# Residual rows, normalisation, router and slot places of two token tiles computed inside the attention loop of a one-core tower kernel, and the slot table written by 4-byte scatters

## What is computed

```python
h = softmax(coeff_weight[x]) @ (bases + lang_bias) * 16 + 0.1 * lang_bias[2]       # (4, 1024, 256)
p = layernorm(h) @ Wv.T + bv                                # q = k = v = p, 16 heads of 16
h = h + (softmax(p @ p.T / 4) @ p) @ Wo.T + bo              # attention over 1024 keys
xn = layernorm(h)                                           # eps 1e-5
logits = xn @ router                                        # 8 experts
top2, idx = top_k(logits, 2); w = softmax(top2)
out = h + sum over the two: w * ((silu(xn @ w13[e][:, :512]) * (xn @ w13[e][:, 512:])) @ w2[e])
```

## Time and profile before

| | us |
|---|---|
| median of 3 runs | 1062.44 (1062.09 to 1062.56) |
| the profiled execution's own time | 1064.38 |
| its span, first to last instruction | 1060.9 |
| mean granted clock of PE | 0.907 |

### The profile page before, as it was taken

The page is one execution under the profiler, slowest core; times in us unless marked ns, Lnnn a source line. Parts: engine busy times, 40 slices in busy tenths (PEclk is TensorE's granted clock), DMA queues, the critical chain, the costliest instruction groups (busy, mean ns, idle before and its releaser), DMA issues. The chain is left out here.

```text
span 1060.9 us, 18151 instructions
## 1 busy us (share of the span) xinstructions
PE 878.6 (83%) x6059; PEld 408.3 (38%) x6095; DVE 448.8 (42%) x1019; ACT 631.4 (60%) x671; POOL 281.7 (27%) x224
## 2 busy tenths in 40 slices
PE   4384899999989989999987896054999999999996
PEld 2270112112112112211214785022666666666664
DVE  5074222221212222222113899994455444554443
ACT  0124999999999999999996066301333332333322
POOL 7621000000000000000000045901555555555553
PEclk9675999999999999999999955555999999999999
DMA  1000000000000000000000477600233333333332
GB/s 22 2 12 1 1 1 1 2 1 1 1 1 1 1 2 1 1 1 1 1 1 9 151 240 208 187 2 18 50 60 55 58 56 59 60 55 60 51 48 30
DMA packets 34649, 40.00 MB, mean 38 GB/s; under 512 B 8848, under 2 KB 30370, under 8 KB 34595
## 3 DMA queue, kind: packets, MB, share of 16 engines
q0 software_dynamic: 14176, 17.45, 11.0%
q1 hardware_dynamic: 20418, 21.84, 7.0%
HBM read 22.46 MB, written 17.33 MB: 38 GB/s over the span
## 5 line engine op out<-in xcount | busy, mean ns | idle before, releaser
L679 ACT ACTIVATE h<-PS 128x1536 f32<-128x1536 f32 x342 | 464.1, 1487 | 15.6 <-PE PS L620 11.7
L630 PE MATMUL PS<-h,va 128*32 128x512 f32 x2048 | 275.6, 610 | 5.8 <-DVE acc_s L721 5.3
L874 POOL TENSOR_TENSOR w_p<-w_raw,w_p 128x1024 bf16<-128x1024 f32 x24 | 53.2, 2236 | 545.3 <-ACT w_p L880 545.3
L1162 PE MATMUL PS<-w_p,xsT 128*128 x793 | 190.0, 382 | 2.5 <-ACT xsT L1215 0.7
L620 PE MATMUL PS<-qf,ak 32*128 32x512 bf16 x1024 | 134.6, 389 | 46.7 <-ACT h L679 42.9
L620 PEld LDWEIGHTS PS<-qf,ak 32*128 32x128 bf16 x1024 | 33.2, 91 | 283.6 <-ACT h L679 222.8
L1220 ACT ACTIVATE act_s<-PS 128x512 f32<-128x512 f32 x69 | 41.3, 598 | 154.7 <-PE PS L1162 154.7
L1125 POOL DMA_INDIRECT out<-y_s,idx_tok x68 | 107.7, 1584 | 54.7 <-issue 47.8
L1162 PEld LDWEIGHTS PS<-w_p,xsT 128*128 128x128 f16 x828 | 81.5, 98 | 86.2 <-issue 5.2
L1111 POOL DMA_INDIRECT xs<-xrows,idx_tok x70 | 73.2, 1046 | 129.5 <-DVE weight L1259 85.3
L1179 PE MATMUL PS<-w_p,hidT 128*128 x828 | 101.7, 273 | 0.3 <-DVE hidT L1278 0.3
(11 more groups left out here) (259 smaller groups left out, 865.1 us busy)
## 6 DMA issues: line engine op xcount, KB each, us to landing
w_raw<-w SPq DMA_DIRECT2D x24, 512.0 KB, 4.8
out<-h SPq DMA_DIRECT2D x8, 512.0 KB, 2.9
xrows<-x_parts SPq DMA_DIRECT2D x8, 512.0 KB, 4.3
xs<-xrows,idx_tok POOLq DMA_INDIRECT x70
out<-y_s,idx_tok POOLq DMA_INDIRECT x68
cw<-coeff,xi POOLq DMA_INDIRECT x32
wvT_s<-wvT SPq DMA_DIRECT2D x1, 256.0 KB, 3.0
woT_s<-woT SPq DMA_DIRECT2D x1, 256.0 KB, 3.2
```

The lines of the kernel that those rows point to most:

```text
L630: last = pe.matmul(PS[32 * slot:32 * slot + 32, ACC, :], g.va[:, KT * (grp // HG) + kt, c, :], prob[:, (4 * quad + slot) % (RING * WIDE), ...
L679: act.activation(prob[:, at:at + n, :].rearrange("p n q -> p (n q)"), PS[:, buf:buf + n, :].rearrange("p c q -> p (c q)"), ACT.Exp).then_i ...
L874: pool.tensor_tensor(pieces[n][2], raw(n), pieces[n][1], ALU.subtract).then_inc(w_lo, 1)
L1162: last = pe.matmul(PS[:, up_bank(k) + half, :], xsT[:, k, 2 * a + c, :], g.w13_p[:, w, c, ds(e, 1), FF * half:FF * half + FF].rearrange("p ...
```

## The change

`residual_phase` and `routing_phase` are gone. Their work for the two tiles of a finished group (`tile_of`) is done while the next group's exponentials run:

- PE gets, in `after`, `turn` (two transposes), `tile_rows` (for each tile two float32 matmuls, now 264 columns: 256 of the residual row and the 8 logits, for which the router is folded into `pair` and `resid` in `weights_phase`) and `rank` (two bf16 matmuls of 16 columns).
- DVE gets `place_blocks`, `copy_rows`, `choose`, `normalise` (the reciprocal root by shifts and three Newton steps), `rank_out` and `weigh`. Their program order is fixed: `normalise` stands behind the second half of `query_features`, and the copy `acc_s` behind `weigh`.
- ACT gets one small exponential per group, `gap_exp`, at a fixed place between two units; it waits for `normalise`.
- POOL gets, per group, the cast and the subtraction of one piece of w13 and four indirect scatters of 128 numbers of 4 bytes each into a table in DRAM (`note`). SP loads the next piece after the rows of the group before are ready.
- After the last group the same steps run once more, then `tiles_out`, one gather of the table, `flags_out` and a transpose. The 8 pieces of w2 are cast and subtracted there.
- `g.more` is made from the counts: it is 1 if there are more than 68 tiles, or if for any expert fewer than 128 of its choices come from the first two batches, or its last tile begins before the end of these. Tokens of an expert now stand in their own order.
- In `weights_phase` the constant rows move into `resid`, and a pair product has 264 columns instead of twice 256. `z_blk` is a sixteenth in size.

```diff
             def after(quad):
                 grp, at = quad // GQUADS, quad % GQUADS
-                if at == 2 and grp >= 1:
-                    fold(grp - 1)
-                if at in (5, 9) and grp + 1 < GROUPS:
-                    query_product(grp + 1, int(at == 9))
+                if grp >= 1:
+                    if at == 1:
+                        fold(grp - 1)
+                    if at == 3:
+                        turn(grp - 1)
+                    if at in (5, 7):
+                        tile_rows(grp - 1, int(at == 7))
+                if at in (8, 10) and grp + 1 < GROUPS:
+                    query_product(grp + 1, int(at == 10))
+                if at == 13 and grp >= 1:
+                    rank(grp - 1)
...
+            def note(grp):
+                pool.wait_ge(pos_ready, grp + 1)
+                for k in range(2):
+                    for kk in range(2):
+                        pool.indirect_dma_start(g.slots, bass.IndirectOffsetOnAxis(
+                            pos_i[:, grp % 2, 2 * k + kk:2 * k + kk + 1].bitcast(U32), 0),
+                            g.pair_no[:, tile_of(grp, kk), k:k + 1], None,
+                            bounds_check=TROWS * P - 1, oob_is_err=True).then_inc(noted[grp % 2], 16)
...
+            pool.memset(z_blk[:], 0.0).then_inc(blk_zeroed, 1)
+            pool.wait_ge(g.table_blank, 16 * (TROWS // P))
+            for grp in range(GROUPS):
+                pool.wait_ge(w_in[grp % WB], 16 * (grp // WB + 1))
+                pool.tensor_copy(pieces[grp][1], raw(grp)).then_inc(w_hi, 1)
+                low(grp)
+                if grp >= 1:
+                    note(grp - 1)
+            for n in range(W13, W13 + WB):
+                low(n)
+            note(GROUPS - 1)
+            for n in range(W13 + WB, W13 + WB + 2):
+                low(n)
+            pool.wait_ge(row_ready, 1)
+            for k in range(2):
+                pool.wait_ge(noted[k], 64 * (GROUPS // 2))
+            pool.indirect_dma_start(table_s[:], None, g.table,
+                                    bass.IndirectOffsetOnAxis(row[:].bitcast(U32), 0),
+                                    bounds_check=TROWS - 1, oob_is_err=True).then_inc(table_in, 16)
+            for n in range(W13 + WB + 2, len(pieces)):
+                low(n)
 
         @block.scalar
         def _(act):
+            gap_units = {(GITEMS * (grp + 1) + 4 * 14) // WIDE: grp for grp in range(GROUPS - 1)}
+
+            def gap_exp(grp):
+                act.wait_ge(gap_ready, grp + 1)
+                act.activation(gap[:, 1, :], gap[:, 0, :], ACT.Exp).then_inc(gap_done, 1)
...
             for u in range(UNITS):
...
+                if u in gap_units:
+                    gap_exp(gap_units[u])
+            act.wait_ge(summed, ITEMS // 4)
+            act.wait_ge(w_hi, W13)
+            for n in range(W13, W13 + WB):
+                high(n)
+            gap_exp(GROUPS - 1)
+            for n in range(W13 + WB, len(pieces)):
+                high(n)
...
+            def load(n):
+                if n >= WB:
+                    sp.wait_ge(w_lo, n - WB + 1)
+                sp.dma_start(raw(n), pieces[n][0]).then_inc(w_in[n % WB], 16)
...
+            for grp in range(GROUPS):
+                load(grp)
+                if grp >= 1:
+                    store(grp - 1)
+            for n in range(W13, len(pieces)):
+                load(n)
+            store(GROUPS - 1)
...
+            def choose(grp):
+                logit = h1s[:, grp % 2, :, D:DE]
+                dve.wait_ge(h_copied, 2 * grp + 2)
+                for kk in range(2):
+                    last = dve.max(top[:, kk, :], logit[:, kk, :])
+                link(last)
+                for kk in range(2):
+                    last = dve.max_index(top_i[:, kk, :], top[:, kk, :], logit[:, kk, :])
+                link(last)
+                link(dve.tensor_copy(top_f[:], top_i[:, :, 0:2].rearrange("p t k -> p k t")))
+                link(dve.tensor_tensor(picked[:], g.iota_e.unsqueeze(1).to_broadcast([P, 4, E]),
+                                       top_f[:].rearrange("p k t -> p (k t)").unsqueeze(2).to_broadcast([P, 4, E]), ALU.is_equal))
+                dve.tensor_tensor(chosen[:], picked[:, 0:2, :], picked[:, 2:4, :], ALU.add).then_inc(chosen_ready, 1)
...
+            def normalise(grp):
+                h = h1s[:, grp % 2, :, 0:D]
+                for kk in range(2):
+                    last = dve.bn_stats(stats[:, kk, :], h[:, kk, :])
+                link(last)
+                dve.tensor_tensor(mean[:], stats[:, :, 1], stats[:, :, 4], ALU.add)
+                dve.tensor_tensor(var[:], stats[:, :, 2], stats[:, :, 5], ALU.add)
+                link(dve.tensor_tensor(spread[:], stats[:, :, 1], stats[:, :, 4], ALU.subtract))
+                link(dve.tensor_tensor(spread[:], spread[:], spread[:], ALU.mult))
+                link(dve.tensor_scalar(spread[:], spread[:], 0.25, EPS, ALU.mult, ALU.add))
+                link(dve.scalar_tensor_tensor(var[:], var[:], 1.0 / D, spread[:], ALU.mult, ALU.add))
+                link(dve.tensor_scalar(seed[:], var[:].bitcast(I32), 1, None, ALU.logical_shift_right))
+                link(dve.tensor_scalar(y[:].bitcast(I32), seed[:], -1.0, 1597463007.0, ALU.mult, ALU.add))
+                for scale in (1.0, 0.25, 0.0625):
+                    link(dve.scalar_tensor_tensor(t1[:], y[:], scale, y[:], ALU.mult, ALU.mult))
+                    link(dve.tensor_tensor(t1[:], t1[:], var[:], ALU.mult))
+                    link(dve.scalar_tensor_tensor(y[:], t1[:], -3.0, y[:], ALU.add, ALU.mult))
+                dve.tensor_tensor(spread[:], top[:, :, 1], top[:, :, 0], ALU.subtract)
+                link(dve.tensor_scalar(rstd[:], y[:], -0.125, None, ALU.mult))
+                dve.tensor_tensor(gap[:, 0, :], spread[:], rstd[:], ALU.mult).then_inc(gap_ready, 1)
+                link(dve.scalar_tensor_tensor(mean[:], mean[:], -0.5, rstd[:], ALU.mult, ALU.mult))
+                if grp >= 2:
...
+                for kk in range(2):
+                    last = dve.tensor_scalar(xn[:, kk, :], h[:, kk, :], rstd[:, kk:kk + 1], mean[:, kk:kk + 1], ALU.mult, ALU.add)
+                link(last)
+                link(dve.tensor_copy(rows_h[:, grp % 2, :, 0:D], xn[:]))
+                dve.tensor_tensor(rows_h[:, grp % 2, :, D:2 * D], xn[:], rows_h[:, grp % 2, :, 0:D], ALU.subtract)
+
+            def weigh(grp):
+                dve.wait_ge(gap_done, grp + 1)
+                w = rows_f[:, grp % 2, :, D:XW]
+                link(dve.tensor_scalar(even[:], gap[:, 1, :], 1.0, None, ALU.add))
+                link(dve.reciprocal(w[:, :, 0], even[:]))
+                dve.scalar_tensor_tensor(w[:, :, 1], gap[:, 1, :], -1.0, w[:, :, 0], ALU.add, ALU.mult).then_inc(rows_ready, 1)
...
+            def rank_out(grp):
+                now, then = run[:, grp % 2], run[:, (grp + 1) % 2]
+                dve.wait_ge(rank_mm, grp + 1)
+                link(dve.tensor_tensor(now[:, 1, :], now[:, 0, :], PS[:, UB, TOT:TOT + E], ALU.add))
+                dve.tensor_tensor(then[:, 0, :], now[:, 1, :], PS[:, UB, TOT + E:TOT + 2 * E], ALU.add)
+                dve.tensor_tensor(place[:].rearrange("p t e -> p (t e)"), PS[:, UB, TRI:TRI + 2 * E],
+                                  now.rearrange("p t e -> p (t e)"), ALU.add).then_inc(rank_read, 1)
+                dve.wait_ge(rank_read, grp + 1)
+                link(dve.tensor_tensor(prod[:], picked[:].rearrange("p (k t) e -> p k (t e)", k=2),
+                                       place[:].rearrange("p t e -> p (t e)").unsqueeze(1).to_broadcast([P, 2, 2 * E]), ALU.mult))
+                link(dve.reduce_sum(pos[:], prod[:].rearrange("p k (t e) -> p (k t) e", e=E), X))
+                if grp >= 2:
+                    dve.wait_ge(noted[grp % 2], 64 * (grp // 2))
+                dve.tensor_copy(pos_i[:, grp % 2, :], pos[:]).then_inc(pos_ready, 1)
+                if grp == GROUPS // 2 - 1:
+                    dve.tensor_copy(mid[:], then[:, 0, :])
+
...
+                link(dve.tensor_tensor(few[:, 0, :], mid[0:1, :], g.expert_base[0:1, :], ALU.subtract))
+                dve.tensor_scalar(few[:, 1, :], few[:, 0, :], float(P), None, ALU.is_lt)
+                link(dve.scalar_tensor_tensor(few[:, 2, :], tiles[0:1, :], -float(P), few[:, 0, :], ALU.mult, ALU.add))
+                link(dve.tensor_scalar(few[:, 2, :], few[:, 2, :], -float(P), None, ALU.is_gt))
+                link(dve.tensor_tensor(few[:, 1, :], few[:, 1, :], few[:, 2, :], ALU.max))
+                dve.tensor_reduce(few[:, 0, 0:1], few[:, 1, :], X, ALU.max)
+                link(dve.tensor_scalar(few[:, 0, 1:2], first[2][0:1, E - 1:E], float(USUAL), None, ALU.is_gt))
+                link(dve.tensor_tensor(few[:, 0, 2:3], few[:, 0, 0:1], few[:, 0, 1:2], ALU.max))
+                dve.tensor_copy(g.more[:], few[:, 0, 2:3])
...
+            dve.wait_ge(blk_zeroed, 1)
             for grp in range(GROUPS):
                 if grp >= 1:
```

(10 more changed lines are left out.)

645 lines of the change are left out of this document (273 added, 372 removed).

## The result

The changed kernel takes 1099.59 us (median of 4 runs, 1097.82 to 1100.51) against 1062.26 us before: a ratio of 1.035, 95% interval 1.0332 to 1.0367, slower by 3.5%. The forecast was 1055 with a range of 1030 to 1080. The profiled execution has a span of 1096.1 us, 35.2 more than before.

| stretch (us) | before | after | difference | forecast |
|---|---|---|---|---|
| start to the first copy of sums | 128.67 | 145.28 | +16.6 | 0 |
| first to last copy (attention) | 441.0 | 539.3 | +98.3 | +93 |
| last copy to the experts' first gather | 158.6 | 46.5 | -112.1 | -122 |
| first gather to the end | 332.6 | 365.0 | +32.4 | +22 |

A forecast was written before the change was run, and what follows sets the result against it. ACT's exponentials were taken to bound attention, by little, with routing a stretch without exponentials. Tail -122, attention path +77, clock +16 and experts +22 gave -7 us: 1055 us against the median, range 1030 to 1080.

The forecast's parts named there:

- the likeliest case: The forecast's main case without rivals, chance 0.50: 1040 to 1069 us from its terms' bounds.
- Nothing elsewhere: Added steps of `weights_phase` and `tokens_phase` hide behind POOL's 32 gathers; other start changes balance within 1 us.
- In between it costs nothing: Expert stage: each scatter waits for the one before, but its 3.5 us fit under the 4.56 us pitch.
- rival of scatters one apart: Expert stage: landing, signal and wait exceed the 4.56 us pitch, so every tile lasts longer; 44 us, 1099, chance 0.08.
- The tail: After the last sums: 34.5 us replace the 156.7 us routing stretch, -122 us (bounds -126 and -120).
- if all do: Tail: all of DVE's some 25 small operations collide with POOL, so it ends at about 36 us.
- The path through DVE's order: Attention: ACT's gap exponential waits for DVE's chain, 5.4 us a group for 14 groups; +77 us in all.
- clock 1.15 a group: Attention: PE's granted clock falls after its pauses in most groups; +16 us, between 0 and 14 x 2.
- port rival: Attention: POOL's cast and subtraction fall into `choose` and `normalise`, 2 us a group; 1083 us, chance 0.12.
- clock holds: Attention: PE's gaps stay just short enough that its clock does not fall; 1039 us, chance 0.20.
- light chain: Attention: `normalise` takes half, the gap does not wait, only PE's fullness counts; 988 us, chance 0.05.
- flag stays 0: Expert stage: `g.more` stays 0, so the long path is not taken; 1033 us, chance 0.05.

The follow-up runs named there:

- e9: The changed kernel timed again without any edit: 1082.38 us, ratio 1.0221 against the kernel before.
- e7: The changed kernel, but ACT copies the low halves of the eight w2 pieces and POOL subtracts none (another output): 1076.49 us, ratio 1.0134.
- e17: e11 with flag 0, 68 tiles two apart, added start steps behind `m_blk`, and ACT copying w2's low halves instead of POOL subtracting: 978.52 us.
- e15: e11 with flag 0, 68 tiles two apart, added start steps behind `m_blk`, pieces 19 and 20 cast before the last gap exponential: 993.22 us.
- e5: The changed kernel plus twelve zero-weight matmuls behind `rank` in groups 1 to 14, filling PE's pause: 1070.75 us, ratio 1.0083.
- e4: The changed kernel with the gap's exponentials, `weigh` and row stores one group later, two w2 loads ahead of group 14's store: 1071.76 us, ratio 1.0092.
- e8: e4 with the copy of the group's sums ahead of the last part of `normalise` and of `rank_out`: 1024.27 us, ratio 0.9638.
- e11: e8 with the tail reordered: last four scatters behind two subtractions instead of three, w2 loads and row stores in another order: 1022.56 us, ratio 0.9646.
- e16: e15, but SP has the last two loads of w2 ahead of the store of the last rows: 988.47 us, ratio 0.9315.
- e1: The changed kernel with `g.more` set to 0, so 68 scatters run two apart: 1063.73 us, ratio 1.0012.
- e6: The changed kernel with one square-root round in `normalise` instead of three (another output): 1075.21 us, ratio 1.0112.

## Why the prediction was wrong, point by point

**Sum and sign.** Of 42 us between -7 and +35.2, the start has 16.6, the experts 10.4, the tail 9.9 and attention 5.3. Without the stand, as in e9 (span 1080.9), it would still be +20 and the sign wrong. The range was also drawn too tight: the bounds of its terms add up to -23 and +17 around 1055, that is 1032 to 1072 for the likeliest case, where the text says 1040 to 1069, and they allow 1 us for the start and nothing for the scatters' pitch.

**"Nothing elsewhere" failed**, the largest single miss. That the added steps of `weights_phase` hide behind POOL's gathers is right in the nine of 16 profiles in which DVE does not stand: the tokens phase begins at 53.2 to 53.8, as before. In seven DVE stands, and with the change's order of the steps (five of them) the added router products and `m_blk` are late by 9 to 12 us. The term was put at nothing from POOL's length alone; that DVE's queue might pass a fulfilled wait late was no part of it. Another 3.0 (e9) to 4.4 us lie between the tokens phase and the first copy: the second half of the first features took 1.93 and 1.40 where the first took 0.43 and 0.75, with POOL's first cast and subtractions beside it, and the first query product comes 1.5 (e9) or 2.3 us later after the phase's start than before.

**"In between it costs nothing" failed in the expert stage.** This was the rival of scatters one apart, to which I gave 0.08. It had the threshold right (4.56, traffic 3.5 and 1.0 more) and took the traffic too short: landing takes 3.7 to 3.9 and the way to the next scatter 0.87, 4.7. It is a term of 12.3. Four tiles (18.1 for 18.3) and the end (3.2 for 3.5) were right.

**The tail was 10 us too short: POOL ends it, and later than counted.** The sum had DVE's last step at 34.5 us behind the last sums and the gather 2.0 behind it, as before (726.27 to 728.28). What came last was POOL. Its last subtraction ended at 39.4, which is 4.9 more, and the gather came 7.1 behind that, which is 5.1 more; 5.4 of the 7.1 are the DRAIN.

POOL's own end was counted at 30.7 and came 8.7 later, for two reasons that the trace shows. First, the gap was ready at 22.9 instead of 16.8, and the casts and subtractions from piece 19 on stand behind it: the two tiles' matmuls ran at a granted clock of 0.50 (2.6 us), and two small DVE steps took 1.79 and 1.97 us beside a subtraction instead of 0.17 (3.4). Second, the load of piece 22 was there 7.8 us after its issue, not 4.8 (3.0).

A wait that I had not counted is the landing of the scatters. In the changed kernel it holds POOL for 1.7 us, which its later wait for piece 22 would have taken in any case; it sets the tail in e7 and e17 alone. The Trainium skill ("DMA: Bandwidth & Descriptors", section "Anatomy of one DMA — SWDGE (gpsimd) path") gives about 2.0 us as the fixed part of such a transfer; here the gather behind the four scatters begins 9.4 us after the last of them (e7), and the row decides. For the table I had 2.9; its landing took 5.3 (e7), and 3.7 to 6.9 in the other profiles.

Seven DVE steps of the tail stand beside the eight subtractions, which is near the "if all do" case. The Trainium skill's rule on VectorE and GpSimd ("SBUF — State Buffer", section "Who interferes with whom") agrees with the 7.00 us of one two-column step with two SBUF inputs beside three subtractions (e15).

**Attention was right in mechanism.** The path through DVE's order: second query product 22.5 to 23.2 after the copy (22.8), gap ready 29.9 (29.7), path 5.83 a group (5.4), clock 1.15 a group (1.14, taken from the middle of 0 to 28, so that this one fits so well is partly luck). POOL's work fell between the copies and the features, so the port rival did not occur there. The rivals "clock holds" and "light chain" fell; e5 shows what the first would have given, 14 to 16 us. The rival "flag stays 0" fell with the 72 scatters. What I did say, that `rank_out` and `weigh` stand only 1.4 us behind, e4 shows at work: one wait gone, the next one 2.1 us long and with a clock fall of its own.

**What stays open:** what DVE stands for at the start. The trace shows no instruction fetch in that time, and one and the same kernel has the stand in one execution and not in another. Open too is why POOL's DRAIN ends 5.4 us behind a subtraction here and 0.06 us in the kernel before. The block now also holds indirect transfers on POOL's queue, which the routing block had not; no run tests that.

## What to carry to other kernels

Work that is put beside a full engine was paid here by the order of the queues more than by its length: look for the first instruction that makes the full engine wait, and then for what is queued behind it on the other engines, since that is the next wait. Here the same work cost 98 us with the exponential of the gap waiting for this group's chain and the copy of sums behind all of it. It cost 34 us with the exponential one group later and the copy ahead of the chain's last part (e8: 475.5 from first to last copy against 441.0). A wait just shorter than another does not count until the longer is gone; then it is the one that sets the time (e4).

A version for use is e11: it keeps the rule of the flag and takes 1022.56 us, 3.5% under the kernel before. e16 takes 988.47, but its short path was set by hand for these inputs.

## What the runs showed of the hardware that I had not expected

- POOL's queue has a DRAIN at the end of its block, and the next stage begins 0.42 to 0.43 us after it in all 18 profiles of changed kernels. Where POOL's last work is a subtraction (16 of them: the changed kernel, e1 to e6, e8 to e16) it ends 5.4 us behind that, so the stage begins 5.81 to 5.82 us behind it, even when every other engine had been done for over 8 us (e15). Where the last work is the table's gather (e7, e17) it ends 2.70 us behind the landing. In the kernel before it ended 0.06 us behind a subtraction.
- Between 20 and 52 us, with 32 gathers being issued, DVE passed waits for PE up to 29 us after PE had made their inputs (22.2 to 51.47), in seven of 16 executions, and in none of two with the gathers held back. In the kernel before ACT passed one about 15 us late (35.6 to 50.82).
- The gather that waits for four scatters of 128 words each began 8.0 (e4) to 9.4 us (e7) after POOL was through with the last, wherever POOL had stood for it by over 1 us.
- More work made the kernel faster (e5, -13.5 us from first to last copy), and less work in front of a wait gave back half of its length (e6), both through the clock.
